# A depthwise convolution with its taps contiguous in SBUF, and an MLP whose second chunk is loaded an image earlier

## The reference, cut to what matters

```
local = conv_depthwise_7x7(x, conv_w)                  # layer 0, 384 channels
x = x + proj(attention(q(layernorm(x)) + layernorm(batchnorm(local)), k, v))
y = conv_depthwise_7x7(x, dw_w) + dw_b                 # layer 1
y = gelu(layernorm(y) @ w1 + b1)                       # 384 -> 1536
nx = norm(y over the pixels) / mean of the norms       # needs a whole image
y = grn_g * (y * nx) + grn_b + y
out = x + (y @ w2 + b2)                                # 1536 -> 384
```

## Time and profile before

| | |
|---|---|
| median of 3 runs | 5748.92 us (5747.1 to 5751.15) |
| the profiled execution's own time | 5749.09 us |
| its span, first to last instruction | 5747.1 us |
| mean granted TensorE clock | 0.979 |
| first conv | about 2 to 355 us of the span |
| second conv | about 4283 to 4653 us |
| MLP | about 4655 to 5747 us |

### The profile page before, as it was taken

The page is one execution under the profiler, slowest core; times in us unless marked ns, Lnnn a source line. Parts: engine busy times, 40 slices in busy tenths (PEclk is TensorE's granted clock), DMA queues, the critical chain, the costliest instruction groups (busy, mean ns, idle before and its releaser), DMA issues. The chain is left out here.

```text
span 5747.1 us, 95795 instructions
## 1 busy us (share of the span) xinstructions
PE 5415.1 (94%) x31248; PEld 5149.3 (90%) x31248; DVE 3777.1 (66%) x5909; ACT 3952.3 (69%) x5653; POOL 2084.5 (36%) x1028
## 2 busy tenths in 40 slices
PE   7879989999999999999999999999878889999999
PEld 6779978999999999999999999999877778888888
DVE  4456658777777777777777777777444445555645
ACT  6655546888888888888888888888626754434343
POOL 0003334666666556666655666666300000000000
PEclk9999998999999999999999999999999999999999
DMA  4458862213131221312222131221274531111111
GB/s 121 117 140 267 258 207 38 50 30 55 31 55 31 43 43 30 55 31 49 36 37 49 31 55 30 43 43 30 83 261 113 117 64 38 42 38 42 41 34 46
DMA packets 639648, 419.84 MB, mean 73 GB/s; under 512 B 490353, under 2 KB 620081, under 8 KB 629553
## 3 DMA queue, kind: packets, MB, share of 16 engines
q1 hardware_dynamic: 611312, 379.21, 28.5%
q10 hardware_dynamic: 27840, 34.37, 1.7%
HBM read 252.72 MB, written 160.43 MB: 72 GB/s over the span
## 5 line engine op out<-in xcount | busy, mean ns | idle before, releaser
L845 POOL TENSOR_TENSOR a_e_lo<-a_e_full,a_e_hi 128x768 fp32r<-128x768 f32 x864 | 1924.7, 2228 | 1343.0 <-ACT a_e_hi L855 1290.3
L918 DVE TENSOR_REDUCE a_mx_part<-a_ps_m 128x2 f32<-128x768 f32 x1700 | 1628.4, 958 | 743.2 <-PE a_ps_m L980 715.5
L886 ACT ACTIVATE a_e_full<-a_ps_s 128x768 f32<-128x768 f32 x1728 | 1405.2, 813 | 497.2 <-PE a_ps_s L998 431.4
L855 ACT ACTIVATE a_e_hi<-a_e_full 128x768 fp32r<-128x768 f32 x1728 | 1449.0, 839 | 0.0
L998 PE MATMUL a_ps_s<-a_q,a_k_hi 113*128 113x384 f32 x3456 | 1171.2, 339 | 8.3 <-issue 6.6
L998 PE MATMUL a_ps_s<-a_q,a_k_lo 113*128 113x384 f32 x3456 | 1167.6, 338 | 0.0
L1012 PE MATMUL a_ps_o<-a_e_hi,a_v 128*97 128x384 f32 x3456 | 919.6, 347 | 5.1 <-ACT a_o_t L861 3.8
L980 PE MATMUL a_ps_m<-a_k_hi,a_q 112*128 112x384 f32 x3400 | 883.4, 341 | 33.7 <-DMA a_q<-q_lo 26.4
L1012 PE MATMUL a_ps_o<-a_e_lo,a_v 128*97 128x384 f32 x3456 | 884.3, 337 | 7.6 <-issue 7.6
L911 DVE TENSOR_TENSOR a_e_lo<-a_e_full,a_e_hi 128x768 fp32r<-128x768 f32 x864 | 831.9, 963 | 36.6 <-ACT a_e_hi L855 36.6
L998 PEld LDWEIGHTS a_ps_s<-a_q,a_k_hi 113*128 113x128 f32 x3456 | 651.3, 188 | 38.7 <-issue 17.6
(11 more groups left out here) (146 smaller groups left out, 7271.3 us busy)
## 6 DMA issues: line engine op xcount, KB each, us to landing
local<-c_res ACTq DMA_DIRECT2D x192, 168.0 KB, 2.3
v<-n_v SPq DMA_DIRECT2D x24, 1152.0 KB, 6.3
a_v<-v SPq DMA_DIRECT2D x32, 864.0 KB, 14.5
a_k_hi<-k_hi SPq DMA_DIRECT2D x63, 432.0 KB, 6.8
a_k_lo<-k_lo SPq DMA_DIRECT2D x63, 432.0 KB, 15.5
c_band_raw<-in_taps SPq DMA_DIRECT2D x768, 24.0 KB, 2.4
c_x_raw<-in_x_conv SPq DMA_DIRECT2D x96, 144.0 KB, 2.2
n_xc<-in_x SPq DMA_DIRECT2D x24, 576.0 KB, 6.3
```

Of the source, the lines that this page charges most:

```text
L845: pool.tensor_tensor(e_lo[:, e], e_full[:, e], f32(e_hi[:, e]), ALU.subtract).then_inc(lo_pool, 1)
L855: act.activation(e_hi[:, slot(par, n)], e_full[:, slot(par, n)], ACT.Copy).then_inc(e_hi_made, 1)
L886: act.activation(e_full[:, slot(par, n)], ps_s[:, n % 2, :, 0:CHUNK], ACT.Exp, scale=float(HD) ** -0.5).then_inc(e_made, 1)
L918: dve.tensor_reduce(mx_part[:, par, t, 2 * pair:2 * pair + 2], max_bank(h, u), AX.X, ALU.max).then_inc(mx_red[u % 2], 1)
```

## The change

The raw band tile swaps two axes, so that the 192 floats of one partition's taps lie side by side in SBUF as they do in HBM. The DMA's destination becomes one run of 768 bytes for each partition instead of six of 128 bytes. ACT's `band_hi` and DVE's `band_lo` read the tile through a rearranged pattern in runs of 32 floats; what they write is as before.

In the MLP a second chunk gets a place of its own in `hid`; its load is issued in `results(b)` of the image in front, behind the store of chunk 4, and the wait for the stores moves to the load of chunk 2. The transposes of a second chunk now wait for the last sums, which share their PSUM. The middle third of `x_hi` moves from ACT to DVE (`x_mid`). At a chunk's last step ACT makes the next chunk's outer thirds ahead of gelu f = 11 instead of behind it, as soon as the last matmuls that read the old ones are done, and DVE makes all of `x_lo` ahead of the squares of f = 11, behind its wait for that gelu.

```diff
-        band_raw = sb("band_raw", [P, 3, 6, PC, PS])
+        band_raw = sb("band_raw", [P, 3, PC, 6, PS])
...
-                    sp.dma_start(band_raw[rows, k, :, c, :], taps[g, rows].rearrange("p (o s) -> p o s", s=PS)).then_inc(tap_in[k], 16)
+                    sp.dma_start(band_raw[rows, k, c].rearrange("p o s -> p (o s)"), taps[g, rows]).then_inc(tap_in[k], 16)
...
-                act.activation(band_hi[:, k], band_raw[:, k], ACT.Copy).then_inc(band_hi_made, 1)
+                act.activation(band_hi[:, k], band_raw[:, k].rearrange("p c o s -> p o c s"), ACT.Copy).then_inc(band_hi_made, 1)
...
-                dve.tensor_tensor(band_lo[:, k], band_raw[:, k], f32(band_hi[:, k]), ALU.subtract).then_inc(band_lo_made, 1)
+                dve.tensor_tensor(band_lo[:, k], band_raw[:, k].rearrange("p c o s -> p o c s"), f32(band_hi[:, k]), ALU.subtract).then_inc(band_lo_made, 1)
...
-        first_raw = hid[:, 0:CT, CHUNK:2 * CHUNK]
+        early_raw = [hid[:, 0:CT, (c + 1) * CHUNK:(c + 2) * CHUNK] for c in range(2)]
         def raw_of(u):
 
-            return io if u % NCH else first_raw
+            return io if u % NCH > 1 else early_raw[u % NCH]
...
-                if c == 1:
+                if c == 2:
                     at_least(sp, stored, b * NCH * 16)
...
+                    if c == NEXT_X and b + 1 < nb:
+                        raw((b + 1) * NCH + 1)
...
-                if b:
-                    raw(b * NCH + 1)
...
+            def x_highs(u):
+                at_least(act, x_free, u)
+                for t in (0, 2):
+                    x_high(u, t)
+
             def up(b):
                 for c in range(NCH):
                     u = b * NCH + c
-                    if c:
-                        act.wait_ge(x_free, u)
-                        for t in range(CT):
-                            x_high(u, t)
                     for f in range(FT):
                         n = c * FT + f
+                        if c + 1 < NCH and f == FT - 1:
+                            x_highs(u + 1)
                         act.wait_ge(h_done, b * NF + n + 1)
...
+            def x_mid(u):
+                at_least(dve, x_free, u)
+                dve.wait_ge(full_made, u * 3 + 2)
+                dve.tensor_copy(x_hi[:, 1], full[:, 1]).then_inc(x_mid_made, 1)
...
-                    if c:
-                        for t in range(CT):
-                            x_low(u, t)
...
+                        if c + 1 < NCH and f == FT - 1:
+                            x_mid(u + 1)
                         dve.wait_ge(h_made, b * NF + n + 1)
                         at_least(dve, sq_made, b * NF + n)
                         part = hid[:, f, c * CHUNK:(c + 1) * CHUNK]
+                        if c + 1 < NCH and f == FT - 1:
+                            for t in range(CT):
+                                x_low(u + 1, t)
...
             def tokens(u):
                 pe.wait_ge(raw_in, landed(u))
+                if u % NCH == 1:
+                    at_least(pe, y_made, u // NCH * NC3)
```

More of the change, by code:

```diff
@@ L1197, in mlp_stage @@
             "to_tok", "stats", "sd_made", "rs_made", "normed", "to_ch", "full_made", "eps_made"))
-        x_free, x_hi_made, x_lo_made = sem("x_free"), sem("x_hi_made"), sem("x_lo_made")
+        x_free, x_hi_made, x_mid_made, x_lo_made = sem("x_free"), sem("x_hi_made"), sem("x_mid_made"), sem("x_lo_made")
         h_done, h_made, sq_made = sem("h_done"), sem("h_made"), sem("sq_made")
@@ L1349, in down @@
                         affine((b + 1) * NCH, NEXT_CH[f])
-                    if b + 1 < nb and c == NEXT_X and f in X_AT:
+                    if b + 1 < nb and c == NEXT_X and f in X_AT and X_AT[f] != 1:
                         x_high((b + 1) * NCH, X_AT[f])
@@ L1383, in normal @@
                                   ALU.subtract, ALU.mult).then_inc(normed, 1)
+            def x_mid(u):
+                at_least(dve, x_free, u)
+                dve.wait_ge(full_made, u * 3 + 2)
+                dve.tensor_copy(x_hi[:, 1], full[:, 1]).then_inc(x_mid_made, 1)
             def x_low(u, t):
-                dve.wait_ge(x_hi_made, u * CT + t + 1)
-                at_least(dve, h_done, u * FT)
+                if t == 0:
+                    at_least(dve, h_done, u * FT)
+                if t == 1:
+                    dve.wait_ge(x_mid_made, u + 1)
+                else:
+                    dve.wait_ge(x_hi_made, u * 2 + t // 2 + 1)
                 dve.tensor_tensor(x_lo[:, t], full[:, t], f32(x_hi[:, t]), ALU.subtract).then_inc(x_lo_made, 1)
@@ L1469, in down @@
                         if ahead is not None and c == NEXT_X and f in X_AT:
+                            if X_AT[f] == 0:
+                                x_mid(ahead)
                             x_low(ahead, X_AT[f])
@@ L1480, in _ @@
             dve.wait_ge(par_in, 96)
+            x_mid(0)
             for t in range(CT):
@@ L1513, in up @@
                         for t in range(CT):
-                            if f == 0 and j != 1:
-                                pe.wait_ge(x_lo_made if j else x_hi_made, u * CT + t + 1)
+                            if f == 0 and j == 2:
+                                pe.wait_ge(x_lo_made, u * CT + t + 1)
+                            if f == 0 and j == 0:
+                                if t == 1:
+                                    pe.wait_ge(x_mid_made, u + 1)
+                                else:
+                                    pe.wait_ge(x_hi_made, u * 2 + t // 2 + 1)
                             last = pe.matmul(ps_h[:, f % 3, 0:CHUNK], wp[:, t, f * P:(f + 1) * P], xp[:, t],
```

## The result

The changed kernel takes **5656.45 us**, the median of three runs (5652.59 to 5658.5), against 5748.92 before: a ratio of 0.9838 [0.9816, 0.986], 92.5 us less, where 98 were forecast. Its profiled execution took 5656.45 us, with a span of 5654.5.

The account below looks back on a forecast made before the run. No engine was full; a conv loop of waits through the tap DMAs set the pace. Conv 63, early second chunk 26 and chunk starts 9 summed to 98 us off 5749.1: 5651 us, own range 5630 to 5680, wider range 5615 to 5705.

Parts of the forecast that it names:

- Loop A: Conv: x_lo through SP's image and tap DMAs, band copy and x_hi back to x_lo; 3.42 us a group, binding before.
- loop B: Conv: matmuls through ACT's finish, band copy, x_hi and x_lo back to matmuls; 3.125 us a group, binding after; gain 57 us.
- The issue's price: Conv tap DMAs: one run per partition issues in 0.432 us instead of 0.60, landing 1.9 us after its start.
- Rival 1: Conv tap DMAs: an issue costs the same however few its pieces, so the conv gains nothing; 5714 us, chance 0.13.
- The broken read: Conv band copy and band_lo: reading the raw band in strided runs of 32 floats was costed at nothing.
- rival 2: Conv band copy: the broken read takes 2.0 us instead of 0.85, making the kernel slower; 5776 us, chance 0.03.
- Disturbances and roundings: Conv: 12 us regained from delayed loads, 8 us lost to ACT's twelve weight roundings between finish and band copy.
- the first loads: Start of each conv: the first loads are 0.8 us shorter, 2 us in all.
- The second chunk: MLP image boundaries: the early load removes PE's 6.6 us wait and 2.1 us of slow clock, 26 us for three images.
- The chunk starts: MLP: twenty chunk starts each 0.43 us sooner, with x_lo behind gelu late next; 9 us, at most 24.
- rival 3: MLP second chunk: the wait only changes its name, to the sums or a late load; 26 us lost, 5677, chance 0.08.
- Rival 4: Conv and MLP: disturbances vanish, roundings hide, x_lo is on time; 147 us, 5602, half the extra 5626; chance 0.06.

Follow-up runs that it names:

- The pair with the late finish: ACT finishes each conv group one group later: on the kernel before 5729.93 us, ratio 0.999; on the changed kernel 5630.84 us, ratio 0.9816.
- the conv of before: The kernel before with only the change's MLP lines, its conv lines untouched: 5700.4 us, ratio 0.9939.
- the taps first: The changed kernel with SP issuing a group's four tap DMAs ahead of its image load: 5631.56 us, ratio 0.9822.
- the kernel with all three edits: The changed kernel with finish one group later, tap DMAs ahead of the image's, and x_lo ahead of the wait for gelu: 5547.76 us, ratio 0.9673.
- the two further cuts: The changed kernel with finish one group later (5630.84 us) or tap DMAs ahead of the image's (5631.56 us); both together 5567.66 us, ratio 0.9706.

## Why the prediction was right

**Loop A bound, loop B took over: right, and the size nearly so.** The forecast was 3.42 and 3.125 us a group; undisturbed it is 3.39 before and 3.13 after, and the waits changed from the DMA to the finish. The pair with the late finish separates the two: cutting B gives 0.1% on the old kernel and brings the new one to 2.98 and 3.02 us, the forecast's 6.04 / 2 for the new loop A. The step is a little smaller than forecast: 0.26 us a group in the traces of the result, 50 us of the 57, and 0.24 in the experiments (3.37 to 3.13), 46 us.

**The issue's price: right.** 423 ns for 432, landing 2.0 us for 1.9. That the row was so near is partly luck: the first conv's image load, also one run for each of 128 partitions, is issued in 0.33 us. But a still cheaper issue would have changed nothing, since loop B stands. Rival 1, no gain from fewer pieces, is out. The Trainium skill, page "DMA: Bandwidth & Descriptors", section "Anatomy of one DMA", on which it leaned, counts about 2.0 us of fixed cost for a DMA on GpSimd's path, beside a term for its bytes; the landing after the change agrees (2.0), but before it, with six pieces a partition, a DMA of the same bytes took 2.4, and an issue 180 ns more of SP's time.

**The broken read costs nothing: right.** 0.854 us for 0.845, against the 2.0 of rival 2. The Trainium skill, page "SBUF — State Buffer", section "Door 1: The DMA port swizzle (why `[64,N]` ≈ `[32,N]`)", says that accesses within one 16-byte line run at full rate and that crossing to a new line costs; runs of 32 floats fill whole lines as an unbroken read does, so it would have set this price at nothing, and the trace agrees.

**Disturbances and roundings: mis-sized by little, and their split is open.** Forecast were 12 us back from disturbances and 8 lost to weight roundings, 4 net, and 2 for the first loads. The first x_lo came 1.2 us earlier in the first conv (13.4 to 12.2) and 1.9 in the second (10.9 to 9.0), 3 in all. The disturbances with the roundings fell from 0.235 to 0.195 us a group on average, 0.04 x 190 = 8 us where 4 were forecast; but the undisturbed step, 3.39 - 3.13 = 0.26, makes 50 us of the 57, since the tenth percentile before lies 0.03 under the loop's 3.42. So the border between the terms is uncertain by some 7 us, and their sum, 50 + 8 + 3 = 61, is what the stages show (61.6). The 8 us did not repeat: in the experiments the disturbances are 0.18 us a group in the conv of before and 0.17 to 0.18 in the changed one, so nothing clear came back, and the conv edit gained 53 us by the traces and 56.4 by the medians. That the 63 were met so closely in the result is thus partly luck: the step came out smaller than forecast, and a longer execution of the conv before made up for it. And the issue of 7.1 us, by which the prediction showed the disturbances, is not part of the steady pace: it stands among the first loads of the second conv. No run tells disturbances and roundings apart: the second conv holds eight roundings, the first four, but the difference of their paces is 0.01 us in the change and 0.04 with the taps first. What the runs do show is how a disturbance is absorbed: not by B being 0.1 us longer than A, which left 0.2 us a group standing, but by more slack. With the taps first 0.08 is left, at the same undisturbed pace.

**The second chunk: right.** 26.1 us for 26, no wait for the load or for the sums took its place (rival 3), and the clock stays at 1.00 over all three boundaries.

**The chunk starts: right, in the size and in what is late next.** 0.45 us for 0.43 each. x_lo behind the gelu was named as next, with 24 us as the end if it were not late. Moving it ahead gave 16 us by the trace on top of the 9, 25 in all.

**The sum.** 63 + 26 + 9 = 98 forecast; measured 92.5, with 4.5 of the difference in stages that the change doesn't touch. Rival 4, a larger gain, fell because the disturbances stayed and x_lo was late; what it hoped for had to be made by hand, in the kernel with all three edits.

## What to carry to other kernels

When no engine is full, draw every loop of waits, divide its length by the iterations that it spans, and expect a cut of the longest to be worth only the distance to the next: here 0.295 us a group by the drawing and 0.24 to 0.26 measured, and by the length of the convs the two further cuts were worth 14 and 19 us alone but 84 together. Where a queue serves a loop, let the long leg wait for the earliest thing that allows it, and keep slack in that loop, since it pays for disturbances that the loop's own length doesn't show. And an operation that another engine needs should not stand behind a wait that it doesn't need itself: one such place, repeated 20 times, was worth 16 us in the MLP.

## What the runs showed of the hardware that was not expected

**The program's own fetch disturbs the issues of the data's DMAs.** Each 16 KB that q8 brings for PE in the convs comes with a tap issue of 0.7 to 2.4 us instead of 0.60. One case in the kernel before, in the timeline of SP's queue, four issues in 4.17 us instead of 2.51:

```profile
140.64 4.17 SPq L186 DMA_DIRECT2D c_band_raw<-in_taps  x4
```

and the DMA view of 141.2 to 143.2 us:

```profile
q8 instruction: 1, 0.02, 5.8%
```

The Trainium skill, page "Runtime: NRT & Kernel Launch", section "Instruction fetch mechanics", says that the refill in blocks of 16 KiB is mostly hidden. The trace agrees with the block's size, but SP's issues beside it pay, 27.4 us in the two convs before, 0.14 us a group, and where the loop has no slack the conv pays with them. How a packet on q8 lengthens an issue of SP, no run shows.

**The price of a tap issue fell with its pieces, and did not fall with its partitions.** 0.60 us for 32 partitions of six pieces of 128 bytes, 0.42 for 32 of one, and 0.42 for 16 of one. But the number of pieces alone does not set a price. The image load of the second conv writes four pieces of 288 bytes in each of 128 partitions, and the load of v in the attention 18 pieces of 384 bytes (source views of L180 and L791 before, the first from 4280 to 4660 us):

```profile
L180 SPq DMA_DIRECT2D c_x_raw<-y x96: 360/366/627, 4283.3 to 4639.1; - x96
```

```profile
L791 SPq DMA_DIRECT2D a_v<-v x31: 380/381/425, 890.8 to 3931.5; - x31
```

Both are issued faster than a tap of one piece. What makes six pieces of 128 bytes dear, no run shows.

**A rounding copy on DVE is cheap.** The copy of 384 elements takes 0.355 us, the subtraction of the same size 0.55 (source views of L1391 and L1400); the prediction had put the copy at 0.56 at most.
